# The last addition of a feed-forward tile as an accumulating transfer from GpSimd's queue, and the input sums of the first stage at the end of VectorE's turn

## The reference, cut to what matters

```
x = x + 0.5 * ffn(layernorm(x))          # first stage
x = x + attention(layernorm(x))          # causal, 4096 x 4096, two batches
x = x + 0.5 * ffn(layernorm(x))          # last stage

ffn(n):  m = k0*n[s-1] + k1*n[s] + k2*n[s+1]        # mix of three neighbours
         nine paths h_e = (m @ W1[e] + b1[e]) @ W2[e] + b2[e]
         e* = argmax(tanh(m @ Wo1 + bo1) @ Wo2 + bo2)
         y = n + h_e*
         return (y - mean(y)) * rsqrt(var(y) + eps) * gamma + beta
```

## Time and profile before

| | before |
|---|---|
| median of three executions | 1445.7 us (1445.36 to 1446.14) |
| profiled execution: its own time | 1444.34 us |
| its span | 1442.5 us |
| granted TensorE clock, mean | 0.982 |
| PE busy | 1335.2 us (93%) |
| VectorE busy | 1181.9 us (82%) |
| ScalarE busy | 922.6 us (64%) |
| GpSimd busy | 328.1 us (23%) |

### The profile page before, as it was taken

One profiled execution on the slowest core, in us unless ns is written; L12 is line 12 of the kernel. 1 busy time (PEld: TensorE's weight loads), 2 busy tenths in 40 slices (PEclk: granted clock), 3 DMA queues, 4 the chain that ended last, 5 costly groups with the idle time before them and its releaser, 6 DMA issues.

```text
span 1442.5 us, 24659 instructions
## 1 busy us (share of the span) xinstructions
PE 1335.2 (93%) x7700; PEld 772.8 (54%) x7700; DVE 1181.9 (82%) x2326; ACT 922.6 (64%) x1717; POOL 328.1 (23%) x359
## 2 busy tenths in 40 slices
PE   3999998898999999999898999999998879999995
PEld 2567766664455454545354455454544346777764
DVE  5999999887787787778877778787778768989986
ACT  5666765366566766566875666767666866667641
POOL 2254543442010000130020101000310004545422
PEclk9899999999999999999999999999999989999998
DMA  5243333310010000002100010000102212333221
GB/s 159 52 126 108 98 119 93 93 44 31 30 45 16 29 15 15 28 17 74 45 15 30 30 45 15 29 30 1 44 1 90 72 32 60 114 107 99 91 81 59
DMA packets 86985, 82.18 MB, mean 57 GB/s; under 512 B 8539, under 2 KB 86884, under 8 KB 86884
## 3 DMA queue, kind: packets, MB, share of 16 engines
q1 hardware_dynamic: 86884, 80.91, 18.7%
HBM read 55.43 MB, written 25.46 MB: 56 GB/s over the span
## 4 chain that ended last, share of the span: by engine, by line
PE 62%; DVE 17%; issue 9%; ACT 7%; POOL 2%; DMA 1%; DVEq 0%; ACTq 0%; POOLq 0%; SPq 0%
PE PS L1641 56%; DVE R L1051 2%; DVE R L1045 2%; PE PS L1739 2%; PE PS L1649 2%; DVE run_max L1039 2%; ACT R L1481 2%; ACT R L1485 1%; DVE x_st L1073 1%; PE PS L1710 1%; DMA R<-in_L_attn_x 1%; DVE R L821 1%; POOL R L612 1%; DVE R L908 1%; ACT R L1440 1%
## 5 line engine op out<-in xcount | busy, mean ns | idle before, releaser
L1641 PE MATMUL PS<-R 128*128 128x512 f16 (+3 forms) x3456 | 720.4, 363 | 35.3 <-DVE R L1051 27.1
L1641 PEld LDWEIGHTS PS<-R 128*128 128x128 f16 (+1 forms) x3456 | 327.1, 98 | 395.3 <-DVE R L1051 53.4
L1051 DVE TENSOR_TENSOR R<-R 128x512 f16<-128x512 f32 (+3 forms) x288 | 188.8, 655 | 96.9 <-ACT R L1485 95.2
L1472 ACT ACTIVATE R<-PS 128x512 f32 (+5 forms) x288 | 160.3, 558 | 157.8 <-PE PS L1641 157.7
L1481 ACT ACTIVATE R<-R 128x512 f32<-128x512 f32 (+4 forms) x288 | 169.6, 589 | 56.0 <-DVE R L1045 55.2
L1641 PE MATMUL PS<-R,w_hi 128*128 128x512 f16 x640 | 196.6, 390 | 4.3 <-DVE R L805 4.3
L1641 PE MATMUL PS<-w_hi,R 128*128 128x256 f16 x1024 | 188.2, 273 | 10.9 <-DVE R L862 10.9
L1485 ACT ACTIVATE R<-R 128x512 f16<-128x512 f32 (+3 forms) x288 | 171.1, 594 | 26.7 <-ACT R L1481 0.4
L1039 DVE TENSOR_TENSOR run_max<-run_max,R 128x512 f32<-128x512 f32 (+3 forms) x272 | 180.8, 665 | 8.4 <-DVE run_max L1039 1.7
L1045 DVE TENSOR_TENSOR R<-R,max_row 128x512 f32<-128x512 f32 (+4 forms) x288 | 186.9, 649 | 0.5 <-ACT max_row L1549 0.5
L579 POOL TENSOR_SCALAR veps<-mv 128x4 f32<-128x4 f32 x48 | 16.4, 342 | 648.0 <-issue 376.9
(11 more groups left out here) (124 smaller groups left out, 1749.9 us busy)
## 6 DMA issues: line engine op xcount, KB each, us to landing
R<-x_scratch SPq DMA_DIRECT2D x48, 512.0 KB, 4.1
x_scratch<-R SPq DMA_DIRECT2D x32, 512.0 KB, 3.2
R<-oh_scratch SPq DMA_DIRECT2D x32, 320.0 KB
R<-in_L_attn_x SPq DMA_DIRECT2D x16, 512.0 KB, 5.6
R<-oh_scratch SPq DMA_DIRECT2D x32, 256.0 KB
out<-R SPq DMA_DIRECT2D x16, 512.0 KB, 3.1
R<-in_L_ffn_W SPq DMA_DIRECT2D x2, 288.0 KB
R<-in_L_ffn_W SPq DMA_DIRECT2D x1, 512.0 KB
```

The source lines that it names most:

```text
L1051: v.tensor_tensor(p_lo[:, i * TT + lo:(i + 1) * TT], pf[:, (i % 2) * TT + lo:(i % 2 + 1) * TT], p_hi[:, i * TT + lo:(i + 1) * TT], ALU.sub ...
L1472: a.activation(cols(ring, ring_m + i * TT + lo, TT - lo), ps_s[:, i, lo:], ACT.Abs, scale=1.0 / (QS * XS * D ** 0.5)).then_inc(abs_done, 1)
L1641: ins = t_.matmul(dst, w, xx, start=start and n == 0, stop=stop and n == last, skip_group_check=skip)
```

## The change

The residual of a tile is no longer added by a DVE instruction. GpSimd issues a transfer from `x_rows(t)` to `n_rows(t)` that adds into its destination, and `x1_done` now counts its landing (16 per tile). The last tile of the last stage is still added by DVE (`by_vector`). In GpSimd's turn the transfer stands behind `residual` and ahead of `norm_scale`; for the first stage's tiles 14 and 15 it stands last. In DVE's turn the input sums of the first stage move from between masked chunks 1 and 2 to the very end, and `input_moments` of both stages goes there too. `added_sums` moves from the end of the turn to where the input sums were, one turn later.

```diff
+        def by_vector(ph, t):
+            return ph == 1 and t == NTT - 1
...  SP, store(t):
-                    sp.wait_ge(x1_done, g + 1)
+                    if by_vector(ph, t):
+                        sp.wait_ge(last_added, 1)
+                    else:
+                        sp.wait_ge(x1_done, 16 * (g + 1))
...  GpSimd, ffn:
+                def residual_added(t):
+                    k = use(ph, t)
+                    pool.wait_ge(scaled_done, k + 1)
+                    pool.wait_ge(xb_done, k + 1)
+                    if k >= 1:
+                        pool.wait_ge(x1_done, 16 * k)
+                    g.dma_start(n_rows(t), x_rows(t), accum_op=ALU.add).then_inc(x1_done, 16)
...  turn(t)
                     if on(t):
                         residual(t)
+                    if on(t - 1) and not by_vector(ph, t - 1) and not left_over(ph, t - 1):
+                        residual_added(t - 1)
                     if on(t + STATS) and not early(ph, t + STATS):
                         (norm_scale)
...
+                    if on(t - 1) and left_over(ph, t - 1):
+                        residual_added(t - 1)
...  GpSimd, attention:
-                    pool.wait_ge(x1_done, NTT)
+                    pool.wait_ge(x1_done, 16 * NTT)
...  VectorE, ffn, added_sums(t):
-                    dve.wait_ge(x1_done, t + 1)
+                    dve.wait_ge(x1_done, 16 * (t + 1))
...  turn(t)
                         masked(t + HIDDEN, 1)
-                    if ph == 0 and rows:
-                        for u in range(SUB):
-                            input_sum(t + STATS, u)
+                    if ph == 0 and 0 <= t - 2 - NT < EARLY:
+                        added_sums(t - 2)
                     if here:
                         masked(t + HIDDEN, 2)
                         masked(t + HIDDEN, 3)
...
                         masked(t + HIDDEN, 4)
-                    if rows:
-                        input_moments(t + STATS)
-                    elif first_of(ph, t):
+                    if first_of(ph, t):
                         first_stats(first_of(ph, t))
                     if last and not left_over(ph, t - 1):
                         result_scaled(ph, t - 1)
...
-                    if last and not left_over(ph, t - 1):
+                    if last and by_vector(ph, t - 1):
                         result_added(ph, t - 1)
-                        if ph == 0 and 0 <= t - 1 - NT < EARLY:
-                            added_sums(t - 1)
+                    if rows:
+                        if ph == 0:
+                            for u in range(SUB):
+                                input_sum(t + STATS, u)
+                        input_moments(t + STATS)
...  VectorE, attention, before the first step:
-                    result_added(0, NTT - 2)
...
-                    result_added(0, NTT - 1)
```

More of the change, by code:

```diff
@@ L214, in macaron @@
         scaled_done, xb_done, x1_done, stored = sem("scaled_done"), sem("xb_done"), sem("x1_done"), sem("stored")
+        last_added = sem("last_added")
         a_hi, a_lo, aT_psum, aT_hi, aT_lo = sem("a_hi"), sem("a_lo"), sem("aT_psum"), sem("aT_hi"), sem("aT_lo")
@@ L828, in result_added @@
                 dve.wait_ge(scaled_done, use(ph, t) + 1)
-                v.tensor_tensor(n_rows(t), n_rows(t), x_rows(t), ALU.add).then_inc(x1_done, 1)
+                v.tensor_tensor(n_rows(t), n_rows(t), x_rows(t), ALU.add).then_inc(last_added, 1)
             def ffn(ph):
```

## The result

| | before | after |
|---|---|---|
| median | 1445.53 us, 4 executions (1444.5 to 1446.14) | 1432.47 us, 4 executions (1431.0 to 1433.6) |
| ratio, 95% interval | | 0.9912 (0.9899 to 0.9925) |
| profiled execution: own time, span | 1444.34, 1442.5 us | 1431.63, 1429.8 us |
| granted clock, mean | 0.982 | 0.989 |

The change made the kernel 13 us faster, 0.9%. The forecast was 1433.6 us, with a range of 1429 to 1442. In the changed kernel L862 has become L883, L829 L850 (the last tile alone), L821 L842, L843 L864, L870 L891, L805 L826, L908 L929, L1641 L1660, L1011 L1032, L1022 L1043, L1036 L1057, L1039 L1060 and L644 L665. The accumulating transfer is issued in L630.

A forecast was written before the change was run, and what follows sets the result against it. PE, busy 93% of the span, was taken as the bound, so DVE work counts only where PE waits. Terms 7.7 + 1.7 + 1.3 + 1.7 - 0.3 = 12.1 us off 1445.7 gave 1433.6 us, range 1429 to 1442.

The forecast's parts named there:

- gaps and clock, turns 1 to 16: First stage: PE's gaps before `path` shrink by 7.7 us; the clock staying up gives another 1.7 us.
- beginning: Turns -2 and -1: moved sums cost 1.45 us, their removal gives back about 1.2; -0.3 us in all.
- start of attention: PE's 1.31 us wait for L1011, behind two removed additions, goes entirely: 1.3 us gained.
- end: Last stage: last addition ends 3.4 us earlier, of which the store chain loses 1.7; 1.7 us gained.
- Steady turns: First stage, turns 4 to 9: DVE's turn 0.26 us longer, within a 0.36 us margin; no gain, no loss.
- rival of a late DVE: Steady turns: DVE overruns its margin; losing 1 us a turn costs 5.8 us, giving 1439.4; chance 14%.
- Late turns: First stage: 2.47 us leaves DVE's loop, so gaps of 3.57 and 2.54 shrink to 1.10 and 0.5.
- Load and input sums have over 11 us: Outside the end, a transfer of 6.0 us is covered; load and input sums have over 11 us.
- A: Time from the end of a tile's scaling to `x1_done`: taken as 6.0 us, bounds 3.2 and 11.2.
- rival of the other sign: GpSimd held by its own transfer issue ahead of `norm_scale`; at 6 us, +19 us, 1452; chance 9%.
- The 5 us of room: GpSimd has some 5 us from scaling to the next turn's end before its issue delays PE.
- Both go, so the whole gap does: Start of attention: both additions ahead of L1011 are removed, so PE's whole 1.31 us gap vanishes.

The follow-up runs named there:

- the three extra sums: Changed kernel with three more unused input sums at the end of DVE's turns 1 to 8 of the first stage; 1436.8 us.
- order-only kernel: Kernel before with only the moved sums and moments and the later `added_sums`, DVE still adding every residual; 1447.63 us, ratio 1.0019.
- transfer-only run: Changed kernel with input sums and moments back at their old places, accumulating transfer and later `added_sums` kept; 1449.9 us, ratio 1.0032.
- the doubled issue: Changed kernel with each accumulating transfer issued as two halves of 256 KB; 1433.71 us.
- the run with the earlier `key_low`: Changed kernel with GpSimd's `key_low` waiting for 15 landed transfers instead of 16; 1431.49 us.
- the query's edit: Changed kernel with query 2's low half ahead of the fourth running maximum at the start of attention; 1430.92 us alone, 1428.47 us combined with two other edits.

## Why the prediction was right

By the profiled executions (1442.5 to 1429.8 us, 12.7):

| term | forecast | measured |
|---|---|---|
| gaps and clock, turns 1 to 16 | 7.7 + 1.7 = 9.4 | 10.26 (234.44 to 224.18 us) |
| beginning | -0.3 | -0.33, and -0.65 that is not the edit's |
| start of attention | 1.3 | 0.37 (904.81 to 904.44 us, all of attention) |
| end | 1.7 | 3.05 |
| sum | 12.1 | 12.7 |

The sum is closer than its terms. Each is off by 0.7 to 1.4 us, two of them each way, and they nearly cancel; that part is luck. So is some of the 12.7: the changed kernel's second profile has a span of 1431.6 us, which would make it 10.9.

- **Steady turns.** Right: 15.55 us from L883 to L883, PE without a gap, and a margin of 0.28 to 0.29 us where 0.36 was worked out. The rival of a late DVE was real and near: the three extra sums and the order-only kernel show what it would have been.
- **Late turns.** Right in place and mechanism: 0.70 and 0.38 us stay where 1.10 and 0.5 were forecast, and the clock did not fall. That is 0.5 us more of idle time (8.25 instead of 7.7), and each gap that closes gives some 0.16 us beyond its shown length. With the clock's 1.7 it makes 10.4; 10.26 were measured. That nothing fell behind the short gaps agrees with the order-only run, where the clock is 1.00 behind 1.11 us and 0.50 behind 2.15. But the 3.57 us of the kernel before left it at 1.00, so the length of the gap alone does not decide, and what does stays open.
- **The load.** "Load and input sums have over 11 us" held: no wait for the load is left. But the prediction booked the moved sums for the 0.46 us gap of turn 3 alone. The transfer-only run shows what they are worth beside a transfer, 19 us in turns 2 to 9, which the prediction had not weighed.
- **A.** 6.0 was taken, 4.9 measured. It had been set near the load (5.6) and lies between store and load. So the end loses 0.5 us to the store chain and not 1.7; the last addition's own gain, 3.4 forecast, was 3.5 (229.19 to 225.66 us from the last stage's first result). The Trainium skill, page DMA: Bandwidth & Descriptors, section on the anatomy of one DMA, gave an estimate of 3.2 us, or 4.4 with the second read; the latter is close to the 4.6 from issue to landing. SP's issues of the last stores, of the kernel before and of the one after:

```profile
1431.90 7.66 SPq L478 DMA_DIRECT2D out<-R  x2
```
```profile
1414.37 12.51 SPq L486 DMA_DIRECT2D out<-R  x3
```

  The last of them ends at 1439.56 and 1426.88, 0.39 and 0.89 us after the last addition's end (1439.17 and 1425.99).

- **GpSimd's issue.** 0.9 us, with 1.94 us idle behind it, so the rival of the other sign was far off. The 5 us of room weren't tried beyond the doubled issue. `neg` took 0.46 us at its new place instead of 2.29.
- **Start of attention.** The wrong step is "Both go, so the whole gap does". The gap for L1011 did go, but the next one grew. The rows of the kernel before, then after:

```profile
322.28 11.11 POOL L644 TENSOR_TENSOR R<-R 128x1024 f16<-128x1024 f32 x5 [7.04 <-DVE R L829]
```
```profile
328.98 5.75 DVE L1039 TENSOR_TENSOR run_max<-run_max,R 128x512 f32<-128x512 f32 x3
```
```profile
336.03 10.22 PE L1641 MATMUL PS<-R 128*128 128x512 f16 x48 [4.11 <-DVE R L1022]
```
```profile
312.96 11.54 POOL L665 TENSOR_TENSOR R<-R 128x1024 f16<-128x1024 f32 x5 [3.74 <-DMA R<-R]
...
317.56 7.48 DVE L1060 TENSOR_TENSOR run_max<-run_max,R 128x512 f32<-128x512 f32 x3
```

  Before, `key_low` started 6.7 us ahead of the three maxima, after it 4.6, since it waits for the last transfer; DVE's maxima stand beside more of it, and PE waits 5.23 instead of 4.11 us. The forecast followed the removed additions to the first gap and stopped there. At attention's first column maximum the changed kernel is 1.5 us ahead (20.52 instead of 22.04 us from the first stage's last result), at the second 0.4 (42.39 instead of 42.79). In its second profile it is 0.6 us behind there (43.36), because the clock was at 0.50 for some 7 us behind the same gap, instead of some 3.5, and the 48 matmuls took 11.19 us instead of 10.21:

```profile
328.99 11.19 PE L1660 MATMUL PS<-R 128*128 128x512 f16 x48 [5.24 <-DVE R L1043]
```

  So of the forecast 1.3 us at most 0.4 is left.

## What to carry to other kernels

Work handed from an engine to a transfer comes back later than it did: before the move, list every queue entry that stands behind its semaphore, here the store, the load behind the store in SP's queue, the sums of that load and the sums of the result, and give each of them room of the landing time (4.9 us here). Two edits that each lose alone (+4 and +2 us, both with the later `added_sums`) can gain 13 together, so a half that measures slower is not evidence against the whole. And where a removed wait is followed by a wait on the same engine, follow the chain to the second one before the first is booked as a gain.

## What the runs showed of the hardware

- A DVE operation with two on-chip inputs and a GpSimd operation beside it slow each other by more than an even share would: a 128 x 128 addition took 2.97 us instead of 0.28, a scaling of four groups 3.77 instead of 1.66, and it was back at 1.67 once GpSimd's `residual` was moved. The Trainium skill, page SBUF — State Buffer, section Who interferes with whom, says that such a DVE operation and a GpSimd instruction that reads the same memory exclude each other; the traces agree.
- An accumulating transfer of 512 KB between two on-chip tiles takes 4.6 us from issue to landing and 0.9 us of GpSimd's own time. Its packets account for 2.8 us, those of a half for 1.55.
- In the beginning the granted clock falls to 0.50 (the level of 1.2 GHz) in some executions, at one of two places. The windows of the kernel before, of the changed kernel's first profile, and of its second:

```profile
32.00:44.00 12.00, 8.74 (x31) 5.03 (x32) 10.96 (x29) 7.59 (x13) 1.86 (x4) 0.50 0.19 51
```
```profile
46.00:54.00 8.00, 6.47 (x36) 3.05 (x33) 8.00 (x16) 4.63 (x6) 0.00 (x0) 1.00 0.16 50
```
```profile
46.00:54.00 8.00, 5.61 (x16) 2.18 (x17) 6.57 (x13) 3.54 (x4) 0.00 (x0) 0.58 0.15 44
```

  Between 32 and 44 us it costs nothing that shows (tile 0's result at 69.50 us), between 46 and 54 it makes tile 0's result 2.6 us later (73.12 instead of 70.48). Neither place is tied to the edit: the changed kernel had no such stretch in its first profile and the later one in its second, and the run with the earlier `key_low`, which begins with the same instructions, had the one from 32 to 44 us. What makes the clock fall at one or the other stays open. Single microseconds were therefore read from intervals of the profiles, not from medians.
- At the end of attention the granted clock is at 0.50 in every profile, but not for the same time: about 14 us in the kernel before and in the changed kernel's first profile, 10 in the second, and 17 in both profiles with the query's edit and in two without it (the halves and the three more sums). Windows inside it, of the changed kernel's two profiles and of the query's edit:

```profile
1163.00:1175.00 12.00, 8.78 (x31) 5.05 (x32) 4.27 (x10) 7.60 (x13) 0.00 (x0) 0.50 0.22 51
```
```profile
1164.00:1173.00 9.00, 4.62 (x18) 2.61 (x18) 4.50 (x10) 5.30 (x9) 0.00 (x0) 0.50 0.17 50
```
```profile
1159.00:1175.00 16.00, 11.21 (x37) 5.83 (x38) 8.27 (x20) 9.59 (x16) 0.00 (x0) 0.50 0.14 39
```

  From attention's last column maximum to the last stage's first result it took 108.10 us in the first, 106.95 in the second and 109.25 with the query's edit. So the total moves by 1 us without any edit. What sets the length of this stretch stays open.
